# A fused four-layer kernel on one core: another hand-written order of its steps, and unread products beside the scores of every batch element but the first

## The reference

```
x = x + L0_attn(layernorm(x))   # state-space scan
x = x + L0_ffn (layernorm(x))   # 16-head causal attention that modulates a gated MLP
x = x + L1_attn(layernorm(x))   # gated linear attention, 4 heads, chunks of 64
x = x + L1_ffn (layernorm(x))   # mixture of 32 experts, 4 chosen for a token
```

## Time and profile before

| | |
|---|---|
| timed runs, median (range) | 3068.35 us (3061.31 to 3069.5) |
| profiled execution | 3051.84 us, span 3049.8 us |
| TensorE busy | 2495.4 us (82%) |
| VectorE busy | 2162.5 us (71%) |
| ScalarE busy | 1368.1 us (45%) |
| GpSimd busy | 676.4 us (22%) |
| line 1561, VectorE scan | 256 x 2301 ns |
| line 1585, VectorE product | 256 x 1248 ns |
| line 1570, VectorE product | 256 x 1244 ns |
| line 1717, VectorE maxima | 176 x 1125 ns |
| line 2152, narrow unread product | 22 x 463 ns |

### The profile page before, as it was taken

One profiled execution on the slowest core, in us unless ns is written; L12 is line 12 of the kernel. 1 busy time (PEld: TensorE's weight loads), 2 busy tenths in 40 slices (PEclk: granted clock), 3 DMA queues, 4 the chain that ended last, 5 costly groups with the idle time before them and its releaser, 6 DMA issues. The chain is left out here.

```text
span 3049.8 us, 36680 instructions
## 1 busy us (share of the span) xinstructions
PE 2495.4 (82%) x12295; PEld 1486.0 (49%) x12295; DVE 2162.5 (71%) x3033; ACT 1368.1 (45%) x2184; POOL 676.4 (22%) x609
## 2 busy tenths in 40 slices
PE   5548898889888988898889888988897878876991
PEld 2335346534653465346535643564445433545771
DVE  4999768885888589968885889588937431334666
ACT  5446346534653465346534653465324233232330
POOL 3002001410141014201410142014202210214551
PEclk7668699879986999799879987999796889967995
DMA  3322121222122212221222122212211831714657
GB/s 126 113 94 88 56 82 57 85 85 82 62 83 81 87 63 82 89 85 59 85 87 81 61 85 85 82 62 85 89 55 49 199 116 50 241 37 134 189 170 293
DMA packets 140453, 297.04 MB, mean 97 GB/s; under 512 B 14416, under 2 KB 83424, under 8 KB 140016
## 3 DMA queue, kind: packets, MB, share of 16 engines
q1 hardware_dynamic: 126448, 256.15, 25.7%
q0 software_dynamic: 13824, 38.55, 3.5%
HBM read 225.11 MB, written 69.54 MB: 97 GB/s over the span
## 5 line engine op out<-in xcount | busy, mean ns | idle before, releaser
L1561 DVE TENSOR_TENSOR_SCAN scan<-scan 128x1024 f32<-128x1024 f32 x256 | 589.1, 2301 | 8.7 <-ACT scan L1283 6.4
L1283 ACT ACTIVATE scan<-scan 128x511 f32<-128x511 f32 x512 | 340.3, 716 | 512.8 <-DVE scan L1561 507.3
L967 POOL DMA_INDIRECT rows_dram<-stage,slot_at x128 | 196.7, 1536 | 1103.8 <-DVE scan L1561 845.7
L2255 PE MATMUL bank<-ident,scan 128*128 128x128 f32 x2048 | 323.9, 315 | 139.4 <-DVE scan L1570 133.9
L2255 PEld LDWEIGHTS bank<-ident,scan 128*128 128x128 f32 x2048 | 283.3, 165 | 200.1 <-DVE scan L1570 130.3
L1585 DVE TENSOR_TENSOR scan<-scan 128x1024 f32<-128x1024 f32 x256 | 319.6, 1248 | 17.9 <-PE bank L2255 16.2
L1570 DVE TENSOR_TENSOR scan<-scan 128x1024 f32<-128x1024 f32 x256 | 318.6, 1244 | 0.0
L2330 PE MATMUL bank<-rest 32*128 32x384 f32 (+3 forms) x1024 | 288.0, 677 | 15.6 <-DVE rest L1717 15.4
L1717 DVE TENSOR_REDUCE rest<-bank 128x2 f32<-128x1024 f32 (+3 forms) x176 | 196.4, 1125 | 101.9 <-PE bank L2335 90.3
L1327 ACT ACTIVATE rest<-bank 128x2048 f32<-128x2048 f32 (+3 forms) x128 | 157.3, 1229 | 99.9 <-PE bank L2356 99.8
L1752 DVE TENSOR_TENSOR rest<-rest,bank 128x512 f32<-128x512 f32 x64 | 44.0, 687 | 197.6 <-PE bank L2128 156.3
(11 more groups left out here) (386 smaller groups left out, 4237.8 us busy)
## 6 DMA issues: line engine op xcount, KB each, us to landing
scan<-bc_dram SPq DMA_DIRECT2D x256, 512.0 KB, 3.7
wslot<-wt SPq DMA_DIRECT2D x64, 384.0 KB
rows_dram<-scan SPq DMA_DIRECT2D x32, 670.0 KB
scan<-y_dram SPq DMA_DIRECT2D x32, 512.0 KB, 9.9
rest<-rows_dram SPq DMA_DIRECT2D x108, 134.0 KB
scan<-rows_dram SPq DMA_DIRECT2D x52, 134.0 KB
scan<-wt SPq DMA_DIRECT2D x4, 1536.0 KB, 14.8
wslot<-x SPq DMA_DIRECT2D x8, 512.0 KB, 3.8
```

Of the source, the lines that this page charges most:

```text
L967: g.indirect_dma_start(rows_dram, bass.IndirectOffsetOnAxis(ap=slot_at[:, j:j + 1], axis=0), stage[:, j % NT], None).then_inc(scattered.se ...
L1283: i = a.activation(decay[:, unit % 2, n, 1:], dt[:, c, 1:], ACT.Exp, scale=a_neg[:, c, 2 * pair + n:2 * pair + n + 1])
L1561: d.tensor_tensor_scan(flat, decay[:, unit % 2].rearrange("p n t -> p (n t)"), flat, 0.0, ALU.mult, ALU.add).then_inc(decay_used.sem, 1)
L2255: m = t_.matmul(A.bank(("yT", c))[:, t * P:(t + 1) * P], drive[:, unit % NDRIVE, n, t * P:(t + 1) * P], ident[:, :], is_transpose=True, st ...
```

## The change

Two things change. The dictionary ORDER has other texts for all five engines. And the unread products stand in every turn but turn 0. No other step's code changes, and each column has as many steps as before.

```diff
--- before
+++ after
@@ ORDER, "PE", the head; all five texts are replaced
-        "U1 R165 X6 U2 X1 U1 X5 U2 X2 U1 X2 U13 X1 U2 X3 U3 X2 U1 X1 U11 X4 U1 X1 U1 R2 U1 R3 U1 R8 X1 U3 R5 "
+        "U1 R165 X6 U3 X6 U24 X2 U1 X2 U1 X4 U3 X3 U4 X4 U1 X1 U1 R2 U1 R11 U2 X6 U2 R5 U1 R8 U1 R4 U1 R22 U1 "
...
@@ rest_part of TensorE
                     room(B, turn, ("S", u))
                     b = banks(("S", u))
-                    if isinstance(turn, int) and turn == BATCH - 1:
+                    if turn:
 
 
                         if u == 0:
                             unread(b[:, 0], 3, True)
                         unread(b[:, 1], 1, False)
```

More of the change, by code:

```diff
@@ L99 @@
     "PE": (
[18 rows of a table removed]
[20 rows of a table added]
     ),
     "DVE": (
[19 rows of a table removed]
[18 rows of a table added]
     ),
     "ACT": (
[19 rows of a table removed]
[19 rows of a table added]
     ),
     "POOL": (
[3 rows of a table removed]
+        "U33 R8 X6 R1 X1 R1 X2 R1 X2 R5 X3 R1 U13 R1 X1 U3 X1 R5 X3 R1 U14 R1 X1 U2 X1 R5 X3 R1 U13 R1 X1 U3 "
+        "X1 R5 X3 R1 U14 R1 X1 U2 X1 R5 X3 R1 U13 R1 X1 U3 X1 R5 X5 R1 U16 R6 X2 R1 X28 R1 X20 R4 X5 R1 X3 "
     ),
     "SP": (
[4 rows of a table removed]
[3 rows of a table added]
     ),
```

## The result

The changed kernel takes 3078.95 us (median of five runs, 3074.77 to 3080.52), the kernel before, on the same chip, 3061.31 (3057.02 to 3069.5). The ratio is 1.0052, 95% interval 1.0028 to 1.0077: slower by half a percent, where 3040 us and faster was forecast. The profiled execution has a span of 3072.7 us for 3049.8, 22.9 more.

What follows compares the result with a forecast made beforehand. No single engine bounds the kernel: stretches are TensorE's, VectorE's or nobody's. Turns 1 to 5 -23, turn 0 -3, turns 6 and 7 -2 make -28 us, so 3040 us; range 2982 to 3115.

Steps and rivals of the forecast that it cites:

- The condition on the products: Score stretches, turns 1 to 6: products keep the clock up for the larger part; TensorE 6.5 us saved to 12.2 lost.
- The slower rival: Scores: the clock falls all the same, +7 in each of five turns, +12 in turn 6; +42, 3110 us; chance 0.33.
- Turn 0: First turn, without products, its units spread alike: -3 us, between -8 and +5.
- Scores without them: Scores and maxima of a middle turn: VectorE becomes the bound at 95%, 62.5 us for 58.25, +4.
- Transposed scores: Second stretch of a middle turn: VectorE's work rises to 59 us, at 94% it takes 63: 0.
- MLP and fifth stretch: Middle turn: MLP loses its six TensorE units, -4.6 us; fifth stretch's second-projection products go later, -3.
- Last stretches: Sixth to eighth stretch of a middle turn: two waits fewer, work moved both ways, -1 us.
- Turn 6: Scan units 16 to 30 in one block make attention rest 85 us: 342 us for 300.34, net +42.
- Turn 7: Scores without expert blocks -19, MLP +7, expert blocks spread through the gated attention -32: net -44 us.
- The sum: Whole kernel: -23 for turns 1 to 5, -3 turn 0, -2 turns 6 and 7: -28 us, 3040 us.
- The rule on transposes: Skill page: transposes don't count as TensorE activity for its clock, making the slower case likely; the prediction went by the trace instead.

Runs made afterwards that it cites:

- order_only: The changed kernel with its new order, but the unread products in turn 7 alone, as in the kernel before: 3042.52 us, 0.9942 of the kernel before.
- old_double: Kernel before with turn 7 in the new order, two narrow unread products per unit and the wide group in turns 1 to 7: 2966.53 us, 0.9698.
- seven_only: The kernel before with the new order for turn 7 alone, no added products: 3016.11 us, 0.9877.
- mid_only: The kernel before with the new order up to the MLP of turn 5, unread products in turn 7 alone: 3029.71 us, 0.9890.
- mid_and_six: As mid_only, but turn 6 also in the new order with its block of scan units: 3094.05 us, 1.0110 of the kernel before.
- products_only: The kernel before, in its old order, with the unread products in turns 1 to 7: 3101.55 us, 1.0132.
- best_double: New order except in turn 6, two narrow unread products per unit and the wide group in turns 1 to 7: 3006.80 us, 0.9847 of kernel before.
- six_spread: order_only with turn 6's scan units spread behind value products on TensorE, routing ahead of VectorE's block, ScalarE's decays spread: 2996.13 us, 0.9813 of kernel before.

## Why the prediction was wrong, point by point

- **The condition on the products: wrong, and this is the step that turned the sign.** It took the clock "to be up for the larger part", a range from 6.5 us saved to 12.2 lost for TensorE, and hid the rest under VectorE's bound. The clock was at 0.50 for 31 to 48 of 65 us, over half in turns 1, 2 and 4 (34.1, 47.8 and 37.5 us) and just under it in turns 3 and 5 (30.7 of 64.4). The products cost 3.3 us in the scores and 3.0 ahead of them, 34.4 us by the profiled spans of the changed kernel and order_only, 36.4 by the medians; 3.7 of the 34.4 stand in turn 7 and ahead of turn 0's scores, where the two programs are the same. The forecast had put them at nothing. The warning was on view: turn 7's low 30.7 us with products. The slower rival named this mechanism, and its +42 us were too much: it had TensorE at 74 us in the scores, and 64.4 and 3.0 ahead of them is the most that came (turn 2).
- **Turn 0: -3 forecast, -6.4 in order_only.**
- **Scores without them: right.** +4 was forecast (62.5 us by VectorE's work), +4.2 is the mean of order_only.
- **Transposed scores: 0 forecast, -3.9 measured.** VectorE's share was put at 94%; it was 65.64 of 66.50.
- **MLP and fifth stretch: -7.6 forecast, -9.3 measured** (order_only), for the reason given: the MLP without units takes 49.4 us.
- **Last stretches: -1 forecast, +3.2 measured.** In turns 1 to 4 they take 1.5 us more; the rest of the mean is the end of turn 5, 10 us longer, where the order of turn 6 already begins (10 scan units on VectorE for 7). The scan units that left the MLP stand in the first two stretches. In sum order_only gains 5.9 us a turn for 4.6.
- **Turn 6: +42 forecast, +60.6 in order_only.** This is the second step that failed. The first value product came 80 us after the first transposed scores (85 - 4 = 81 forecast). The 14 units behind it took 55 instead of 40, with two waits of ScalarE of 17.6 us in all among them (last section), and from there to the MLP it was 11 for 16. Scores, MLP to gated attention, and the end took 3 to 4 us each more than counted.
- **Turn 7: -44 forecast, -36 in order_only.** The expert blocks gave back their 25 (MLP to the gated attention's first output: 121.6 us in the changed kernel for 146.1). Of the 19 us of the scores 3.4 came: with blocks gone the clock stood at 0.50 for 41.0 us, and what was saved in work was lost in clock.
- **The sum.** Turns 6 and 7 were put at -2, and are +24.5 without the products. By the profiled spans turns 0 to 5 gained 35.8 us in order_only (26 forecast), the tail lost 24.5 and the products 34.4: 23.1 more, and the span is 22.9 longer. The miss of 26.5 in turns 6 and 7 alone would have left the forecast's 28 at about nothing; the 34.4 of the products make it a loss. The time, 3078.95, lies in the range, on the side that had 0.36.
- **The rule on transposes** (the Trainium skill, "TensorE: Matmul & The Clock Gate", "Part 4: PE-mode transpose") got no run of its own: transposes stand in every score stretch here. The trace of before speaks against it: lines 2115 and 2255 are both transposes, from 1012.85 us on TensorE runs nothing else, and at 1018.40 its clock goes from 0.50 to 1.00 (rows below). In the block of turn 6 they run for 1.97 of each 4.45 us at 0.50 and don't lift it, which fits either.

```profile
1012.85 3.68 PE L2115 MATMUL bank<-ident,rest 128*128 128x128 f32 x16
1016.32 2.95 PE L2255 MATMUL bank<-ident,scan 128*128 128x128 f32 x16
```

```profile
1014.40:1018.40 4.00, 4.00 (x20) 4.00 (x20) 2.50 (x8) 0.00 (x0) 0.00 (x0) 0.50 0.00 0
1018.40:1021.80 3.40, 3.40 (x20) 1.80 (x18) 3.40 (x3) 1.09 (x2) 0.00 (x0) 1.00 0.36 112
```

## What to carry to other kernels

Work that is there only to hold a clock must be enough, or it is pure cost: with the wide group, one product beside each unit lost 1.3%, and two won 1.6% (old_double 2966.5 us for seven_only 3016.1; 1.8% by the ratios). Try the next amount before giving it up, and try it where the other engine isn't the bound: where it is, a held clock has nothing to give. When a new order comes as one piece, join old and new at places where both have done the same steps: here that parted a gain of 32 us of the whole (new up to turn 5, mid_only), one of 39 (turn 7, seven_only) and a loss of 64 (turn 6, mid_and_six against mid_only). The best version found, old_double, takes 2966.5 us (0.9698, 0.9679 to 0.9716), and is ahead of both kernels.

## What the runs showed of the hardware that was not expected

- The same program section has two lengths in one execution: in products_only the scores of five turns take 64 to 66 us and of one 53.9, by where the clock falls and rises (51 to 55 us or 21 at 0.50).
- Two narrow products take 1.03 us at 0.50 and 0.61 at 1.00 (the rows of best_double above), so that the 44 of a turn at 1.00 cost TensorE 13 us, and 22 at 0.50 nearly as much, 11.
- Behind the block of turn 6 two exponentials waited 5.3 and 12.3 us for something that the profile doesn't name, while GpSimd ran its 16 scatters (in order_only 17.6 us in all). In six_spread they aren't there. The cause is open.
